# Four-layer attention kernel: half of the P V key tiles as three fp16 products, and the second output half ahead of the last score block

## The chip, the cores and the metric

The kernel runs on one core of one Trainium2 chip. The metric is the device time of one execution, in microseconds. The core's engines run side by side, each through its own instruction list in order, and wait for one another on semaphores: PE (TensorE), DVE (VectorE), ACT (ScalarE), POOL (GpSimd), and SP, which issues DMAs here.

## What is computed

Four attention layers, each added to the running `x` (4 batches, 512 queries, 256 channels), against one context of 1024 keys and 512 channels. Layers 0, 2 and 3 have 16 heads of 64 channels:

```python
q = hidden_states @ Wq
k = encoder_hidden_states @ Wk
v = encoder_hidden_states @ Wv
logits = jnp.einsum('bhqd,bhkd->bhqk', q, k) * scale
logits = logits + col_bias[None, None, :, :]
probs = jax.nn.softmax(logits, axis=-1)
out = jnp.einsum('bhqk,bhkd->bhqd', probs, v)
out = out @ Wo + bo
out = out + residual
```

Layer 1 is grouped attention (16 heads of 16 channels over 4 key/value heads) with an RMS norm of `x` in front. All of it is float32.

## The kernel before

The unit of work is a block `p`: one batch and two heads of a wide layer (96 blocks in layers 0, 2, 3), or one batch and four heads of layer 1 (16 grouped blocks); N = 112. Every engine has the same loop over slots `s`, written out by hand. A slot computes the scores of block `s`, the second half of P V, the sums and the output of block `s - 1`, and the projections of blocks `s + 1` and `s + 2`. Most slots of wide blocks are "turned" slots; their function is `turned_slot`.

Precision is kept by splitting a float32 number into two fp16 parts (`_h` and `_l`, on ACT the high part, on DVE or POOL the low part) and adding three products, high*high, high*low and low*high. P V alone is a plain float32 product: `attend` multiplies the exponentials `pt` (128 keys x 2 heads x 512 queries, a ring of RING = 6 places in SBUF) by the values `v32`, two heads side by side in the two column halves of the array.

The order in a turned slot of PE: score block 0 (line 981 the bias rows, line 930 the first "opening" maxima product, line 996 the scores of key tiles 0 and 1, line 930 the "closing" maxima product), `attend(s - 1, 1)` (line 1036, tiles 4 to 7), score block 1, sums (line 1056), projections of q, k and v (line 847), score block 2, `project_out(s - 1, 0)`, `attend(s, 0)` (tiles 0 to 3), score block 3, the second half of the next values v1 with the rows of maxima (line 939) in its middle, `project_out(s - 1, 1)`.

Around that order:

- An opening maxima product writes one bank of `ps_sm` and one of `ps_j`; the closing one writes the other bank of `ps_sm`, and with its second matmul the bank that the opening has just used. That matmul waits on `s_max_a`, that is until DVE has reduced the first half of the opening (`maxima`, line 1866: two instructions of 512 columns, each followed by the read-out of the accumulator).
- ACT takes the exponentials (line 1445) from PSUM into `pt`, copies projections out of PSUM (`values`, line 1426; `keys_hi`, line 1405), takes the high part of the summed exponentials (`sums_hi`, line 1452) and spreads the maxima (line 1489).
- POOL adds the eight exponentials of a block into `acc` (`add`, line 711, seven instructions), takes the low part of the sum (`sums_lo`, line 715), and normalizes and splits the output (lines 732 and 737).
- DVE does maxima, reciprocals, the low parts of k and q, and the additions into `x` (`add_out`, line 1911).
- The list `bank_users` gives each user of the two `ps_j` banks its turn; `take` makes PE wait until the reader of the bank's previous user is done.

## Time and profile before

| | us |
|---|---|
| median of 3 runs | 3505.33 (3504.23 to 3508.11) |
| the profiled execution, its own time | 3504.91 |
| its span, first to last instruction | 3502.7 |
| PE busy | 3365.6 (96%) |
| DVE busy | 2354.6 (67%) |
| POOL busy | 2187.3 (62%) |
| ACT busy | 1763.6 (50%) |
| additions of the exponentials, line 711, POOL (1365.5 and 223.2) | 1588.7 |
| P V matmuls of line 1036, PE, 3040 records | 694.2 |

The page gives the busy time of each engine and, for each line, the time that the engine stood idle before it and what ended that idle time. The timeline gives single instructions in order of time. A float32 matmul leaves two records. A matmul's duration includes the way through the array, so the spacing of starts tells what it costs in a row of matmuls.

### The profile page before, as it was taken

The numbers are of one execution on the slowest core, as the hardware profiler recorded it, in microseconds if no ns is written. First come the engines' busy times: TensorE is split into PE (matmuls) and PEld (weight loads), VectorE is DVE, ScalarE is ACT, GpSimd is POOL, SyncE is SP. The second block draws the span as 40 slices with busy tenths as digits, with TensorE's granted clock in tenths as the row PEclk, the third lists the DMA queues.
The fourth block names the chain that finished last, engine by engine and source line by source line (L and its number), as shares of the span: only waits on it lengthen the run. The fifth ranks groups of instructions, "written<-read, shape, count | busy, mean of one in ns | idle before, by whom it ended". The sixth has DMA issues, their size and how long they took to land.

```text
span 3502.7 us, 70154 instructions
## 1 busy us (share of the span) xinstructions
PE 3365.6 (96%) x27438; PEld 1545.0 (44%) x27438; DVE 2354.6 (67%) x4447; ACT 1763.6 (50%) x2228; POOL 2187.3 (62%) x1050
## 2 busy tenths in 40 slices
PE   5999999999997888889999999999999999999998
PEld 2444444444442322234444444444444444444443
DVE  5666666666656788856676666666666666666666
ACT  3444444444455677764444444444444444444444
POOL 5877777767650000028777776777787677767775
PEclk8999999999999999999999999999999999999999
DMA  4000000000000000000000000000000000000000
GB/s 144 10 10 10 1 10 10 9 3 9 6 10 10 9 12 17 17 1 10 10 1 10 10 10 1 10 10 9 3 10 10 1 10 10 10 1 10 3 1 25
DMA packets 50177, 42.09 MB, mean 12 GB/s; under 512 B 4928, under 2 KB 42176, under 8 KB 49856
## 3 DMA queue, kind: packets, MB, share of 16 engines
q1 hardware_dynamic: 49136, 37.08, 3.5%
q8 instruction: 225, 3.69, 0.4%
q14 instruction: 96, 0.79, 0.1%
q10 hardware_dynamic: 720, 0.53, 0.1%
HBM read 32.36 MB, written 2.10 MB: 10 GB/s over the span
## 4 chain that ended last, share of the span: by engine, by line
PE 89%; ACT 3%; DVE 3%; POOL 2%; issue 2%; DMA 0%; ACTq 0%; POOLq 0%; DVEq 0%
PE ps_j L847 39%; PE ps_j L1036 19%; PE ps_st L996 13%; PE ps_sm L930 6%; PE ps_st L981 3%; PE ps_j L1023 3%; ACT pt L1445 2%; PE ps_sm L1010 2%; POOL acc L711 2%; PE ps_j L1056 1%; PE ps_st L930 1%; PE ps_j L939 1%; PE ps_j L1072 0%; PE ps_j L1047 0%; DVE nmg L1856 0%
## 5 line engine op out<-in xcount | busy, mean ns | idle before, releaser
L711 POOL TENSOR_TENSOR acc<-acc,pt 128x1024 f32<-128x1024 f32 x570 | 1365.5, 2396 | 438.8 <-ACT pt L1445 385.1
L1445 ACT ACTIVATE pt<-ps_st 128x1024 f32<-128x1024 f32 x768 | 742.5, 1019 | 447.2 <-PE ps_st L996 435.4
L1036 PE MATMUL ps_j<-pt,v 128*64 128x512 f32 x3040 | 694.2, 598 | 1.4 <-DVE q_l L1771 1.3
L1866 DVE CUSTOM_DVE_ANT_0 ps_sm<-ps_sm,bias_m,nmx 128x512 f32<-128x512 f32 x666 | 480.1, 756 | 274.6 <-PE ps_j L930 227.7
L847 PE MATMUL ps_j<-w_h,ctx_h 128*128 128x128 f16 x3072 | 533.0, 220 | 1.6 <-ACT rinv L1461 1.1
L847 PE MATMUL ps_j<-w_l,ctx_h 128*128 128x128 f16 x3072 | 532.0, 220 | 0.0
L847 PE MATMUL ps_j<-w_h,ctx_l 128*128 128x128 f16 x3072 | 531.9, 220 | 0.0
L1866 DVE CUSTOM_DVE_ANT_0 ps_sm<-ps_sm,bias_m 128x512 f32<-128x512 f32 x486 | 334.4, 706 | 195.6 <-PE ps_j L930 186.4
L732 POOL TENSOR_TENSOR o_un<-o_un,rinv 128x512 f32<-128x512 f32 x111 | 141.6, 1275 | 485.5 <-ACT rinv L1457 294.9
L1036 PEld LDWEIGHTS ps_j<-pt,v 128*64 128x64 f32 x3040 | 201.8, 136 | 407.6 <-issue 369.6
L1903 DVE RECIPROCAL rinv<-rinv 128x256 f32<-128x256 f32 x190 | 331.2, 1745 | 11.2 <-ACT rinv L1461 1.6
L1856 DVE TENSOR_REDUCE nmg<-ps_st 128x2 f32<-128x1024 f32 x248 | 295.8, 1216 | 45.6 <-PE ps_st L930 44.4
L847 PEld LDWEIGHTS ps_j<-w_h,ctx_h 128*128 128x128 f16 x3072 | 301.3, 98 | 54.8 <-issue 40.1
L847 PE MATMUL ps_j<-ctx_h,w_h 128*128 128x512 f16 x800 | 305.1, 381 | 19.2 <-DVE w_l L1771 17.5
L1445 ACT ACTIVATE pt<-ps_sm 128x1024 f32<-128x1024 f32 x256 | 261.3, 1021 | 104.9 <-PE ps_sm L1010 104.8
L930 PE MATMUL ps_sm<-k_h,q_h 64*128 64x512 f16 x1160 | 294.3, 381 | 14.1 <-DVE nmx L1866 11.4
L847 PEld LDWEIGHTS ps_j<-w_l,ctx_h 128*128 128x128 f16 x3072 | 301.6, 98 | 10.7
L847 PE MATMUL ps_j<-ctx_l,w_h 128*128 128x512 f16 x800 | 304.8, 381 | 0.0
L847 PE MATMUL ps_j<-ctx_h,w_l 128*128 128x512 f16 x800 | 304.6, 381 | 0.0
L1405 ACT ACTIVATE k_h<-ps_j 128x512 f16<-128x512 f32 x192 | 114.6, 597 | 373.9 <-PE ps_j L847 373.9
L847 PEld LDWEIGHTS ps_j<-w_h,ctx_l 128*128 128x128 f16 x3072 | 301.6, 98 | 0.0
L996 PE MATMUL ps_st<-q_h,k_h 64*128 64x512 f16 x1488 | 282.4, 376 | 0.0
(182 smaller groups left out, 5490.0 us busy)
## 6 DMA issues: line engine op xcount, KB each, us to landing
w_raw<-wk SPq DMA_DIRECT2D x25, 256.0 KB, 2.8
pt<-ctx_t SPq DMA_DIRECT2D x6, 1024.0 KB, 8.1
w_raw<-wv SPq DMA_DIRECT2D x24, 256.0 KB, 3.6
wo_raw<-wo SPq DMA_DIRECT2D x28, 128.0 KB, 2.0
w_raw<-wq SPq DMA_DIRECT2D x24, 128.0 KB, 2.9
k_h<-k_l SPq DMA_DIRECT2D x72, 32.0 KB, 1.9
x<-x_t SPq DMA_DIRECT2D x4, 512.0 KB, 9.2
acc<-ctx_t SPq DMA_DIRECT2D x2, 1024.0 KB, 8.1
```

The source lines that it names most:

```text
L711: G.tensor_tensor(total, first, pt[:, n % RING, :], ALU.add).then_inc(s_acc, 1)
L732: G.tensor_tensor(o, o, rinv[:], ALU.mult).then_inc(s_o, 1)
L847: done = MM(dst, l, r, start=first and i == 0, stop=last and i == n - 1)
L930: last = MM(dst[h], queries_in(p, tile)[d, t * P:(t + 1) * P], k_h[d, r, half * HALF:(half + 1) * HALF], start=True, stop=True)
L981: MM(ps_st[:, j % 2, j // 2, :], ext_k[rows, buf, kt * P:(kt + 1) * P], ext_q[rows, p % 2, :], start=True, stop=False)
L996: last = MM(ps_st[:, side, h, :], k[d, r, keys], q[d, r, :], start=False, stop=n == 2)
L1036: last = MM(dst[h * HD:(h + 1) * HD, :], values_of(p)[:, kt, h * HD:(h + 1) * HD], pt[:, (units(p) + kt) % RING, h * TQ:(h + 1) * TQ], sta ...
L1405: A(k_h[:, r, keys], bank(f"k{half}", p), ACT.Copy, scale=1 / WS).then_inc(s_k_h, 1)
L1445: A(pt[:, n % RING, :], src.rearrange("p h q -> p (h q)"), ACT.Exp).then_inc(s_exp, 1)
L1856: V.tensor_reduce(nmg[:, half, t, 2 * tile:2 * tile + 2], maxima_in(p, u), AX_X, ALU.max, negate=True).then_inc(s_max, 1)
L1866: last = V.tensor_tensor_reduce(out=src, in0=src, in1=bias_m[:, t, half * HALF:(half + 1) * HALF], scale=-1.0, scalar=nmx[:, 0, t, h:h + 1 ...
L1903: V.reciprocal(r, r).then_inc(s_rinv, 1)
```

## The change

1. In 88 wide blocks (`in_terms`: 1 to 27 and 49 to 109) the key tiles 2, 3, 6 and 7 are multiplied in three fp16 products in place of one float32 product. For that ACT copies the high part of each such exponential tile (`probs_hi`), DVE (tiles 2, 6, 7) or POOL (tile 3) subtracts the low part (`probs_lo`), and half of the values are split too (`values_hi` on ACT, `values_lo` on DVE). The whole tile stands in the place two further in the ring and the two parts in its own, so `place_free` has more to wait for. The exponentials get a factor of 1024 through a bias.
2. `project_out(s - 1, 1)` goes from the end of the turned slot to just before score block 3, with its `add_out`, and the banks of what follows are swapped.
3. Start: the high part of the first two batches of `x` goes from POOL to ACT, DVE does a context split first and the token rows before the rest of its constants, POOL waits for the token rows, and in the first two slots the order of projections differs.
4. End: POOL adds the exponentials of tiles 0 to 3 of the last block, DVE those of tiles 4 to 7, and PE sums both.

```diff
+def in_terms(p):
+    return p >= 1 and turned(p - 1) and turned(p) and turned(p + 1)
@@ bank_users, turned slot
             then("pva", s, 0)
-            opening(3, 1)
-            if nxt:
-                then("v1", s + 1, 0)
-                then("nm0", s + 1, 1)
             if past:
                 then("out1", s - 1, 1)
+            opening(3, 0)
+            if nxt:
+                then("v1", s + 1, 1)
+                then("nm0", s + 1, 0)
@@ take
                     elif before in ("v0", "v1"):
                         pe.wait_ge(s_v_sb, values_before(m) + 1 + int(before[1]))
+                        if in_terms(m):
+                            pe.wait_ge(s_v_l, 2 * terms_before(m) + 1 + int(before[1]))
@@ attend
+                    if parted(p, kt):
+                        n = terms_before(p)
+                        if k == 2:
+                            pe.wait_ge(s_v_l, 2 * n + 1 + part)
+                        if kt == 3:
+                            pe.wait_ge(s_p_l_pool, n + 1)
+                        else:
+                            pe.wait_ge(s_p_l_dve, 3 * n + {2: 1, 6: 2, 7: 3}[kt])
+                        (vh, vl), (ph, pl) = value_parts(p, part), parts(p, kt)
+                        for i, (v, q) in enumerate(((vh, ph), (vh, pl), (vl, ph))):
+                            for h in range(2):
+                                last = MM(dst[h * HD:(h + 1) * HD, :], v[:, k - 2, h * HD:(h + 1) * HD],
+                                          q[:, h * TQ:(h + 1) * TQ], start=False, stop=k == 3 and i == 2)
+                        continue
@@ ACT
+            def values_hi(p, half):
+                act.wait_ge(s_v, values_before(p) + 1 + half)
...
+            def place_free(n, lent=True):
...
+                q, k = owner(n - 2)
+                if lent and not grouped(q) and parted(q, k):
+                    act.wait_ge(s_acc, ADDS * wides(q) + added(k))
+                    if k == 3:
+                        act.wait_ge(s_p_l_pool, terms_before(q) + 1)
+                    else:
+                        act.wait_ge(s_p_l_dve, 3 * terms_before(q) + {2: 1, 6: 2, 7: 3}[k])
+            def probs_hi(p, j):
+                act.wait_ge(s_exp, units(p) + j + 1)
+                place_free(units(p) + j)
+                A(parts(p, j)[0], whole(p, j), ACT.Copy).then_inc(s_p_h, 1)
@@ DVE
+            def values_lo(p, half):
+                dve.wait_ge(s_v_sb, values_before(p) + 1 + half)
...
+            def probs_lo(p, j):
+                dve.wait_ge(s_p_h, 4 * terms_before(p) + {2: 1, 6: 3, 7: 4}[j])
+                hi, lo = parts(p, j)
+                V.tensor_tensor(lo, whole(p, j), hi, ALU.subtract).then_inc(s_p_l_dve, 1)
```

Where the instructions stand now. DVE, from the end of one ordinary slot into the next, before (the two instructions on `ps_sm` and `ps_j` are the opening maxima of score block 0):

```order
L1887 SCALAR_TENSOR_TENSOR ext_q<-ps_j,flags_sb,bias_q 128x512 [waits s_st,s_nm]
L1911 SCALAR_TENSOR_TENSOR x<-ps_j,x 128x512 [waits s_x,s_out]
L1866 ISA ps_sm,nmx<-ps_sm,bias_m 128x512 [waits s_bias_sb,s_max_mm]
L1866 ISA nmx 128x1
L1866 ISA ps_j,nmx<-ps_j,bias_m 128x512
L1866 ISA nmx 128x1
L1866 ISA ps_sm,nmx<-ps_sm,bias_m,nmx 128x512 [waits s_max,s_bias_sb,s_nm16,s_max_mm]
```

and after:

```order
L2035 SCALAR_TENSOR_TENSOR ext_q<-ps_j,flags_sb,bias_q 128x512 [waits s_st,s_nm]
L2047 TENSOR_TENSOR pt<-pt 128x1024 [waits s_p_h]
L1919 SCALAR_TENSOR_TENSOR v<-ps_j,v 128x2x128 [waits s_v_sb]
L2014 ISA ps_sm,nmx<-ps_sm,bias_m 128x512 [waits s_bias_sb,s_max_mm]
L2014 ISA nmx 128x1
L2014 ISA ps_j,nmx<-ps_j,bias_m 128x512
L2014 ISA nmx 128x1
L2047 TENSOR_TENSOR pt<-pt 128x1024 [waits s_p_h]
L2014 ISA ps_sm,nmx<-ps_sm,bias_m,nmx 128x512 [waits s_max,s_bias_sb,s_nm16,s_max_mm]
```

The addition into `x` has gone from between the slots, and the low parts of tile 6 and of the values stand ahead of the opening maxima, the low part of tile 7 behind them.

ACT at the same place, before (line 1445 the exponentials of tiles 6 and 7, then the values, then the exponentials 0 and 1 of the next block, then the high part of the sum):

```order
L1489 ACTIVATE nm_w<-nmx 128x512 [waits s_max,s_nm]
L1445 ACTIVATE pt<-ps_st 128x1024 [waits s_acc,s_pva,s_st] x2
L1426 ACTIVATE v<-ps_j 128x512 [waits s_pvb,s_v]
L1445 ACTIVATE pt<-ps_st 128x1024 [waits s_acc,s_pva,s_st] x2
L1452 ACTIVATE sq<-acc 128x1024 [waits s_sum,s_acc]
```

and after:

```order
L1613 ACTIVATE nm_w<-nmx 128x512 [waits s_max,s_nm]
L1563 ACTIVATE pt<-ps_st,flags_sb 128x1024 [waits s_pva,s_st] x2
L1526 ACTIVATE v<-ps_j 128x2x128 [waits s_pvb,s_v]
L1569 ACTIVATE pt<-pt 128x1024 [waits s_acc,s_pva,s_exp]
L1512 ACTIVATE v<-ps_j 128x256 [waits s_pvb,s_v]
L1569 ACTIVATE pt<-pt 128x1024 [waits s_acc,s_pva,s_exp]
L1563 ACTIVATE pt<-ps_st,flags_sb 128x1024 [waits s_acc,s_p_l_dve,s_pva,s_st] x2
L1576 ACTIVATE sq<-acc 128x1024 [waits s_sum,s_acc]
```

The copy of tile 6 (line 1569) stands behind a copy of values that waits on `s_v`, and the exponentials of the next block wait on `s_p_l_dve` too.

PE from the end of score block 2 to score block 3, before:

```order
L930 MATMUL ps_sm<-k_h,q_h 128x512 [waits s_max_a]
L847 MATMUL ps_j<-o_h,wo_h 128x512 [waits s_v_sb,s_wo_l,s_o_l]
L847 MATMUL ps_j<-o_l,wo_h 128x512
L847 MATMUL ps_j<-o_h,wo_l 128x512
L1036 MATMUL ps_j<-pt,v 64x512 [waits s_max,s_v_sb,s_exp]
L1036 MATMUL ps_j<-pt,v 64x512 x7
L981 MATMUL ps_st<-ext_q,ext_k 128x512 [waits s_exp]
```

and after:

```order
L989 MATMUL ps_sm<-k_h,q_h 128x512 [waits s_max_a]
L906 MATMUL ps_j<-o_h,wo_h 128x512 [waits s_v_sb,s_v_l,s_wo_l,s_o_l]
L906 MATMUL ps_j<-o_l,wo_h 128x512
L906 MATMUL ps_j<-o_h,wo_l 128x512
L1109 MATMUL ps_j<-pt,v 64x512 [waits s_max,s_v_sb,s_exp]
L1109 MATMUL ps_j<-pt,v 64x512 x3
L1105 MATMUL ps_j<-pt,v 64x512 [waits s_p_l_dve,s_v_l]
L1105 MATMUL ps_j<-pt,v 64x512 x5
L1105 MATMUL ps_j<-pt,v 64x512 [waits s_p_l_pool]
L1105 MATMUL ps_j<-pt,v 64x512 x5
L906 MATMUL ps_j<-o_h,wo_h 128x512 [waits s_x,s_wo_l,s_o_l]
```

Four of the eight float32 matmuls have become twelve fp16 ones, the first output half waits on `s_v_l` as well, and the second output half follows at once.

## Rows read from the trace of the kernel before

**Rows 1.** The page, part 1: busy time, share of the span, instructions.

```profile
PE 3365.6 (96%) x27438; PEld 1545.0 (44%) x27438; DVE 2354.6 (67%) x4447; ACT 1763.6 (50%) x2228; POOL 2187.3 (62%) x1050
```

**Rows 2.** Busy time of each engine between 500 and 900 us.

```profile
500.00:900.00 400.00, 400.00 (x3367) 192.42 (x3365) 265.59 (x548) 189.13 (x246) 281.96 (x134) 1.00 0.02 7
```

**Rows 3.** Timeline of PE: start, duration, line, output and inputs, count.

```profile
604.09 0.40 PE L981 MATMUL ps_st<-ext_q,ext_k 32*128 32x512 f16 x4
...
609.11 0.22 PE L847 MATMUL ps_j<-w_h,ctx_l 128*128 128x128 f16 x1
...
609.91 0.40 PE L981 MATMUL ps_st<-ext_q,ext_k 32*128 32x512 f16 x4
...
611.76 0.38 PE L930 MATMUL ps_sm<-k_h,q_h 64*128 64x512 f16 x2
612.07 3.65 PE L1036 MATMUL ps_j<-pt,v 128*64 128x512 f32 x16
615.65 0.40 PE L981 MATMUL ps_st<-ext_q,ext_k 32*128 32x512 f16 x4
...
617.81 0.62 PE L1056 MATMUL ps_j<-sq,ones_h_sb 128*64 128x512 f16 x4
618.37 0.39 PE L847 MATMUL ps_j<-xh,w_h 128*128 128x512 f16 x1
...
642.10 3.65 PE L1036 MATMUL ps_j<-pt,v 128*64 128x512 f32 x16
```

**Rows 4.** Timeline of ACT, in the same slot.

```profile
606.97 1.92 ACT L1445 ACTIVATE pt<-ps_st 128x1024 f32<-128x1024 f32 x2
609.37 0.60 ACT L1426 ACTIVATE v<-ps_j 128x512 f32<-128x512 f32 x1 [0.48 <-PE ps_j L847]
...
613.14 1.06 ACT L1452 ACTIVATE sq<-acc 128x1024 f16<-128x1024 f32 x1
```

**Rows 5.** Timeline of POOL, in the same slot.

```profile
608.05 4.86 POOL L711 TENSOR_TENSOR acc<-acc,pt 128x1024 f32<-128x1024 f32 x2 [3.08 <-ACT pt L1445]
614.27 2.13 POOL L715 TENSOR_TENSOR sq<-acc,sq 128x1024 f16<-128x1024 f32 x1 [1.36 <-ACT sq L1452]
```

**Rows 6.** Timeline of DVE, opening maxima of score block 0.

```profile
610.67 0.70 DVE L1866 CUSTOM_DVE_ANT_0 ps_sm<-ps_sm,bias_m 128x512 f32<-128x512 f32 x1
611.29 0.14 DVE L1866 DVE_READ_ACCUMULATOR2_ANT nmx<- 128x1 f32 x1
611.29 0.73 DVE L1866 CUSTOM_DVE_ANT_0 ps_j<-ps_j,bias_m 128x512 f32<-128x512 f32 x1
```

**Rows 7.** Timeline of all engines at the start, DVE and POOL instructions.

```profile
24.52 5.00 POOL L688 TENSOR_TENSOR ctx_l<-pt,ctx_h 128x2048 f16<-128x2048 f32 x1 [2.94 <-ACT ctx_h L1366]
25.64 4.97 DVE L1826 SCALAR_TENSOR_TENSOR v_rms<-iota_sb,tok_f,v_rms 128x1024 f16<-128x1024 f16 x1
...
29.49 5.03 POOL L688 TENSOR_TENSOR ctx_l<-acc,ctx_h 128x2048 f16<-128x2048 f32 x1
...
30.64 4.96 DVE L1828 SCALAR_TENSOR_TENSOR ext_k<-y_rms,flags_sb,v_rms 128x1024 f16<-128x1024 f16 x1
```

**Rows 8.** Instructions by line: count, min/median/max ns, first and last start.

```profile
L1779 DVE TENSOR_TENSOR ctx_l<-pt,ctx_h x2: 2277/2281/2285, 12.9 to 17.3; 128x2048 f16<-128x2048 f32 x2
L1395 ACT ACTIVATE wo_h<-wo_raw x28: 408/417/417, 97.0 to 3413.1; 128x256 f16<-128x256 f32 x28
```

**Rows 9.** Timeline of PE around two holes, in the grouped layer and at the end.

```profile
1086.84 0.59 PE L847 MATMUL ps_j<-o_h,wo_h 128*128 128x512 f16 x1 [3.92 <-DVE x L1911]
...
1096.47 0.38 PE L1010 MATMUL ps_sm<-q_l,k_h 64*128 64x512 f16 x2
...
3490.12 1.08 PE L1309 MATMUL ps_sm<-acc,ones_sb 128*64 128x512 f32 x4 [2.82 <-DVE acc L2114]
...
3492.22 0.38 PE L847 MATMUL ps_j<-o_l,wo_h 128*128 128x512 f16 x1
```

**Rows 10.** Timeline of PE at the start.

```profile
36.47 1.18 PE L1089 MATMUL ps_j<-ext_k,bias_q 32*128 32x512 f16 x2 [10.58 <-DVE k_l L1771]
```

More of the change, by code:

```diff
@@ L175, in splits_x, with terms_before, parted @@
     return p < N and not grouped(p) and p - STARTS[layer_of(p)] < B
+def in_terms(p):
+    return p >= 1 and turned(p - 1) and turned(p) and turned(p + 1)
+def terms_before(p):
+    return sum(in_terms(i) for i in range(p))
+def parted(p, kt):
+    return in_terms(p) and kt in TERM_TILES
 def place_of(p, u):
@@ L525, in values_of, with whole, parts, value_parts @@
             return v32[:, b if grouped(p) else p % 2]
+        def whole(p, kt):
+            return pt[:, (units(p) + kt + (2 if parted(p, kt) else 0)) % RING, :]
+        def parts(p, kt):
+            both = pt[:, (units(p) + kt) % RING, :].bitcast(F16)
+            return both[:, 0:2 * TQ], both[:, 2 * TQ:4 * TQ]
+        def value_parts(p, half):
+            both = v32[:, p % 2, half * 4 + 2:half * 4 + 4, :].bitcast(F16)
+            return both[:, :, 0:P], both[:, :, P:2 * P]
         def maxima_in(p, u):
@@ L706, in add @@
                         pool.wait_ge(s_pv, KT * (groups(p) + p - G1 - 1))
-                    first = pt[:, (n - 1) % RING, :]
+                    first = whole(p, 0)
                 else:
@@ L710, in add, with probs_lo @@
                     first = total
-                G.tensor_tensor(total, first, pt[:, n % RING, :], ALU.add).then_inc(s_acc, 1)
+                G.tensor_tensor(total, first, whole(p, kt), ALU.add).then_inc(s_acc, 1)
+            def probs_lo(p):
+                pool.wait_ge(s_p_h, 4 * terms_before(p) + 2)
+                hi, lo = parts(p, 3)
+                G.tensor_tensor(lo, whole(p, 3), hi, ALU.subtract).then_inc(s_p_l_pool, 1)
             def sums_lo(p):
@@ L741, in last_slot @@
                 sums_lo(q)
+                for kt in range(1, 4):
+                    n, total = units(N - 1) + kt, acc[:, (N - 1) % 2, :]
+                    pool.wait_ge(s_exp, n + 1)
+                    if kt == 1:
+                        pool.wait_ge(s_sum, N - 2)
+                        first = pt[:, (n - 1) % RING, :]
+                    else:
+                        pool.wait_ge(s_end_add_g, kt - 1)
+                        first = total
+                    G.tensor_tensor(total, first, pt[:, n % RING, :], ALU.add).then_inc(s_end_add_g, 1)
                 normalize(q)
@@ L1124, in wide_slot @@
                     rows_of_reciprocals(s - 1)
[L1125 to L1131 removed]
+                if s < 0:
+                    if s == -1:
+                        project_k(s + 2, 0)
+                    project_q(s + 2, 0)
+                    score_block(2)
+                    project_k(s + 2, 1)
+                else:
+                    if nxt and has_values(s + 1):
+                        project_v(s + 1, 0)
+                    if far:
+                        project_k(s + 2, 1)
+                        if not late_queries(s):
+                            project_q(s + 2, 0)
+                    score_block(2)
                 if past:
@@ L1306, in last_sums @@
             def last_sums():
-                pe.wait_ge(s_end_add, ADDS)
-                for h in range(2):
-                    last = MM(end_sum[h * HD:(h + 1) * HD, :], ones[:, 0:HD], acc[:, (N - 1) % 2, h * TQ:(h + 1) * TQ],
-                              start=True, stop=True)
+                pe.wait_ge(s_end_add_g, 3)
+                for i in range(2):
+                    if i:
+                        pe.wait_ge(s_end_add, 3)
+                    for h in range(2):
+                        last = MM(end_sum[h * HD:(h + 1) * HD, :], ones[:, 0:HD],
+                                  acc[:, (N - 1 + i) % 2, h * TQ:(h + 1) * TQ], start=i == 0, stop=i == 1)
                 last.then_inc(s_end_sum, 1)
@@ L1627, in turned_slot @@
                     group_out(s - 1)
+                if s > 0 and in_terms(s - 1):
+                    probs_hi(s - 1, 7)
                 exponentials_of(0)
@@ L1639, in turned_slot @@
                     queries_hi(s + 2)
-                    if not splits_x(s):
-                        keys_hi(s + 2, 0)
+                if termed:
+                    probs_hi(s, 2)
+                if far and not splits_x(s):
+                    keys_hi(s + 2, 0)
+                if termed:
+                    probs_hi(s, 3)
+                if far:
                     keys_hi(s + 2, 1)
@@ L1644, in turned_slot @@
                     output_hi(s - 1)
+                if nxt and in_terms(s + 1):
+                    values_hi(s + 1, 0)
                 if nxt:
@@ L1654, in turned_slot @@
                 exponentials_of(3)
+                if nxt and in_terms(s + 1):
+                    values_hi(s + 1, 1)
+                if termed:
+                    probs_hi(s, 6)
                 if nxt:
@@ L1931, in _ @@
             link(V.tensor_tensor(tok_f[:], tok_f[:], tok_w, ALU.add))
+            weights_lo(0)
+            for step in range(5):
+                token_rows(0, step)
+            context_lo(1)
             link(V.tensor_scalar(mask_t, mask_t, -1.0, 1.0, ALU.mult, ALU.add))
@@ L1963, in wide_slot @@
                 peak()
-                if far:
+                if s != -1 and far:
                     keys_lo(s + 2, 0)
-                if s == -2:
-                    dve.wait_ge(s_init, 1)
-                    for step in range(5):
-                        token_rows(0, step)
                 peak()
@@ L2002, in turned_slot @@
                 peak()
+                if s > 0 and in_terms(s - 1):
+                    probs_lo(s - 1, 7)
                 peak()
@@ L2027, in turned_slot @@
                 peak()
+                if nxt and in_terms(s + 1):
+                    values_lo(s + 1, 0)
                 peak()
@@ L2036, in turned_slot @@
                     extra_rows(s + 1)
-                if past:
-                    add_out(s - 1, 1)
+                if in_terms(s):
+                    probs_lo(s, 6)
+                if nxt and in_terms(s + 1):
+                    values_lo(s + 1, 1)
             def group_slot(s):
```

169 lines of the change are left out of this document (110 added, 59 removed).

## The prediction

> **What bounds the kernel now.** I read the page's busy times first: PE 96%, DVE 67%, POOL 62%, ACT 50% [rows 1]. Then the windows: between 500 and 900 us PE is busy 400.00 of 400 us at clock 1.00 [rows 2]. The wide blocks therefore run at PE's own pace, and no other engine is late for it. Then one slot in the timeline: P V starts at 612.07 and again at 642.10 [rows 3], so a slot is 30.03 us. In such a slot fewer PE cycles are a gain only as long as nobody else becomes late, so the question for each edit is what it puts in front of an instruction that PE waits for. Last I read the other engines where one slot meets the next [rows 4 to 6].
>
> **P V itself.** Four float32 key tiles take 615.65 - 612.07 = 3.58 us, of which some 0.1 is the change of tile shape, so 0.87 a tile. Two fp16 pairs of the same shape (the sums) take 618.37 - 617.81 = 0.56, that is about 0.22 a pair and a change-over [rows 3]. Three products are 0.65 a tile. Each converted tile saves 0.22, four a block 0.87, and 88 blocks 76 us. The trace shows no step from float32 to fp16 in one tile shape: its cost is between 0 and the 0.1 of a shape change, once for each half, so 0 to 18 us in all. I take 0, the same shape being kept.
>
> **The end of the slot.** The new work on ACT and DVE is small in sum (four copies of 1.06 [rows 4] and about three subtractions of 1.15 a slot, on engines with more than 9 us free), but its place counts. I take the times of the slot at 609.91 and leave out the output half that no longer stands between v1 and the next slot; v1 ends as before (last start 609.11), and the next score block starts near 609.27 instead of 609.91 [rows 3].
>
> - ACT can copy values when v1 is done, at 609.37 [rows 4]. The copy of tile 6 is queued behind `values_hi`, which waits for v1. `values_hi` has 256 columns: 0.42 by the nearest row [rows 8], of which the next instruction overlaps 0.1. `probs_hi` of tile 6 starts near 609.67 and takes the 1.06 of the same shape on line 1452 [rows 4]: 610.73.
> - DVE may then subtract tile 6, near 610.76. It reads two SBUF operands. The trace shows what such an instruction does beside POOL: line 1826 starts at 25.64 while POOL works, and ends at 30.61, 1.1 us after POOL's instruction (24.52 + 5.00 = 29.52); line 1828 does the same against the next one, and that POOL instruction in turn has its end at 34.52 [rows 7]. So DVE waits for the running POOL instruction to end. POOL's two last additions run from 608.05 to 612.91 [rows 5], the second from about 610.48: it is running when DVE comes. DVE gets through at 612.91 and needs 2.28 / 2 = 1.15 [rows 8]: 614.05.
> - `values_lo` reads one operand from PSUM, half of the 0.6 to 0.7 of a 512-column instruction plus its start, 0.4: 614.4.
> - Then the opening maxima: its first half is read out 0.76 after its start [rows 6]: 615.2.
> - The second matmul of the closing product waits for exactly this. PE issues it at 611.76 in a slot that begins at 609.91 [rows 3], so at 611.1 now. It stands until 615.2: a hole of **4.1 us** in every slot that follows a converted block. The rest of PE's queue stands behind it.
>
> The Trainium skill bears on the second step (SBUF — State Buffer, section "Who interferes with whom"): a VectorE instruction with two SBUF inputs and a GpSimd instruction that reads SBUF exclude each other for a whole instruction, and one with at most one SBUF input does not take part. The trace agrees with the first half (4.97 us on a 1.1 us instruction). By the second half `values_lo` and the maxima do not wait for POOL; the sum takes them so, from rows 6, where the maxima run at their own length beside POOL's additions.
>
> **Two more waits in the same slot.** The ring place of exponential 1 of the next block is lent to tile 7 of this one, so that exponential waits for the low part of tile 7. Both opening halves end at 614.4 + 1.5 = 615.9, the low part of tile 7 at 617.05, the exponential (1.02) at 618.1, the high part of the sum at 619.1, and its low part on POOL (2.13 [rows 5]) at 621.25. PE, after the hole: 615.2 + 0.3 + 3.15 of P V + 2.16 of score block 1 = 620.8. It waits 0.5 for the sums. Before, this chain had 1.4 us in hand (614.27 + 2.13 against 617.81). And the first output half takes the bank of v0, which now is free only after `values_lo`, behind the opening maxima of score block 2: these end some 0.1 after the score block does (612.17 against 612.07 in block 0 [rows 3, 6]), and 0.4 more gives a wait of **0.5**. The second output half ahead of score block 3 costs PE nothing: it covers ACT's copy out of the bank that the block needs next.
>
> **The sum.** A slot is 30.03 - 0.87 + 4.1 + 0.5 + 0.5 = 34.3, or 4.2 more; 88 of them are 370 us. In 21 slots (every fourth, with the weight split) the additions of POOL start later and it is a toss-up whether DVE comes first; in 10 more (the first blocks of a layer, where POOL adds `bo`) the wait is about 1.2 shorter: together -29. The two ends: 10.58 us at the start pass while PE waits behind DVE's token rows, which are themselves stretched by POOL [rows 7, 10]; the new order lets them run first and alone. At the end PE waits 2.82 for DVE's additions [rows 9], which are now shared. I take -11 for both, with bounds -3 and -16.
>
> **The clock.** After the hole of 3.92 us at 1086.84 the matmuls of 512 columns take 0.59 to 0.63 in place of 0.38, until 1096.47: the lower of the two levels (1.2 in place of 2.4 GHz) for 9.5 us. After 2.82 us of waiting at 3490.12 they take 0.38 as ever [rows 9]. A hole of 4.1 is on the wrong side. Each drop costs half of the slow stretch: between 0 (it does not come) and 4 us (as at 1086.84) a slot. In full work I expect less than there, about 2.5, not in each slot, and some of it in place of the wait for the sums: 1.25 a slot, 110 us.
>
> 3504.91 + 370 - 29 + 110 - 11 = **3945 us**; the profiled execution stands 0.4 below the median, which changes nothing.
>
> **The rivals.**
>
> 1. *DVE comes ahead of POOL's last addition.* The margin is 610.76 against 610.48, 0.3 us, and rests on durations of instructions that the trace does not show. Then tile 6 is subtracted by 611.9, the opening's first half is read by 613.0, and the hole is 1.9. POOL's addition is pushed back instead, and with it the low part of tile 7 and the sums, a wait of about 0.9 to 1. A slot costs 1.9 + 1.0 + 0.5 - 0.87 = 2.5 more: 3505 + 220 - 11 = 3714; without the wait for the sums 3626. Such a hole is shorter than the 2.82 that left the clock alone.
> 2. *The saving stands (faster).* This needs DVE to be at the opening maxima by 610.4, before PE's closing matmul. The tail between v1's end and that point is 0.3 + 1.06 + 1.15 + 0.4 and would have to fit into 1.0 us: both new instructions on `pt` in less than a third of their nearest rows (1.06 and 2.28 / 2). From there on PE stays full: 3505 - 76 - 11 = 3418, up to 3436 with the type changes. For it speaks only that PE is 96% busy and the others have room.
> 3. *The change does not do what it says:* the fp16 products of the two heads do not run side by side. Then P V takes 12 x 0.22 a half in place of 1.74, 0.9 more, and a slot 2.6 more than in my sum. The pairs of the sums [rows 3] speak against it. It would give about 4150.
>
> **How the numbers follow.** The forecast, a hole near 4 us with the clock somewhere between never and always down, spans 3800 to 4110: 68%. Rival 1, 3626 to 3800: 22%. Rival 2: 5%. No change within 0.2% (7 us, about what a measurement of this kernel can tell) would need the saving and the waits to cancel: 2%. Above 4110, rival 3 or a clock that is down most of the time: 3%. The range of 8 in 10 takes the forecast and most of rival 1: 3650 to 4110. Faster 5%, same 2%, slower 93%.
>
> **What the changed profile would show.** PE's waits: a matmul of the maxima (line 989 there) waiting for DVE's maxima some 88 times, about 4 us each (1.9 in rival 1, none in rival 2). DVE's subtraction of `pt` (line 2047) at 1.15 where POOL is idle and near 3.3 for tile 6. P V's fp16 pairs 0.22 apart. PE's wait for the low part of the sum, and for `values_lo` ahead of the first output half, 0.5 each. PE's clock below 1.00 in the slices of the wide layers. The step most likely to be wrong is the 0.3 us between DVE and POOL; the next is how often the clock falls.

## The result, and the profile after

| kernel | us, median (lowest to highest) | runs | span of the profiled run | mean granted clock |
|---|---|---|---|---|
| before | 3505.49 (3504.23 to 3508.11) | 4 | 3502.7 | 0.992 |
| after | 3935.38 (3934.0 to 3936.35) | 4 | 3932.1 | 0.956 |

After is 1.1226 times before, 95% interval 1.1212 to 1.1239. The change makes the kernel 430 us slower. The forecast was 3945.

The page of after, busy times, against [rows 1]: PE has fewer cycles to do in P V, and yet is busy longer (its clock) and for a smaller share (holes).

```profile
PE 3492.5 (89%) x28146; PEld 1609.8 (41%) x28146; DVE 2800.6 (71%) x4884; ACT 2185.0 (56%) x2758; POOL 2472.3 (63%) x1138
```

PE's waits in after (what PE was about to do, for whom, us in total, times, longest). Of the first, 11.4 us were there in before.

```profile
PE ps_sm L989 <- DVE nmx L2014: 261.5, 96, 3.6
PE ps_j L906 <- DVE v L1919: 29.4, 81, 0.4
PE ps_j L1129 <- POOL sq L762: 21.4, 25, 0.9
```

One boundary between slots, PE first (start, length, engine, line, operation; in brackets the idle time before it and who ended it), against [rows 3]:

```profile
614.47 0.39 PE L1040 MATMUL ps_st<-ext_q,ext_k 32*128 32x512 f16 x4
...
616.32 0.38 PE L989 MATMUL ps_sm<-k_h,q_h 64*128 64x512 f16 x1
620.33 0.60 PE L989 MATMUL ps_sm<-k_h,q_h 64*128 64x512 f16 x1 [3.64 <-DVE nmx L2014]
620.87 3.68 PE L1109 MATMUL ps_j<-pt,v 128*64 128x512 f32 x8
624.33 2.24 PE L1105 MATMUL ps_j<-pt,v 128*64 128x512 f16 x12
```

The same stretch on ACT, DVE and POOL, against [rows 4 to 6]:

```profile
614.57 0.38 ACT L1526 ACTIVATE v<-ps_j 128x256 f16<-128x256 f32 x1 [0.29 <-PE ps_j L906]
614.85 1.05 ACT L1569 ACTIVATE pt<-pt 128x1024 f16<-128x1024 f32 x1
```

```profile
615.93 3.35 DVE L2047 TENSOR_TENSOR pt<-pt 128x1024 f16<-128x1024 f32 x1 [1.95 <-ACT pt L1569]
619.20 0.41 DVE L1919 SCALAR_TENSOR_TENSOR v<-ps_j,v 128x256 f16<-128x256 f32 x1
619.54 0.68 DVE L2014 CUSTOM_DVE_ANT_0 ps_sm<-ps_sm,bias_m 128x512 f32<-128x512 f32 x1
```

```profile
613.35 4.84 POOL L752 TENSOR_TENSOR acc<-acc,pt 128x1024 f32<-128x1024 f32 x2 [2.50 <-ACT pt L1563]
```

The second of POOL's two additions, alone:

```profile
615.85 2.34 POOL L752 TENSOR_TENSOR acc<-acc,pt 128x1024 f32<-128x1024 f32 x1
```

Read from the bottom up. POOL adds tiles 6 and 7 from 613.35 to 618.19. ACT has the high part of tile 6 ready at 615.90. DVE starts to subtract it at 615.93, only 0.08 us after POOL began its last addition, and ends at 619.28, which is 1.1 us after POOL's end. So it was let through when POOL's instruction ended. The same instruction takes 1.21 to 1.22 where no instruction of POOL runs beside it. Only then come the values' low part and the maxima. PE could have issued the second closing product beside the first, at 616.32; it issues it at 620.33, and 4.01 us are lost. The matmuls after the hole take 0.60 in place of 0.38: the clock has fallen to its lower level.

In the next slot, one with a weight split, DVE comes 0.13 us before POOL's last addition. Then DVE keeps its own length, POOL's addition takes 3.31 in place of 2.34 us, and PE's hole is 1.45:

```profile
652.70 1.23 DVE L2047 TENSOR_TENSOR pt<-pt 128x1024 f16<-128x1024 f32 x1 [1.95 <-ACT pt L1569]
```

```profile
652.83 3.31 POOL L752 TENSOR_TENSOR acc<-acc,pt 128x1024 f32<-128x1024 f32 x1
```

The clock by stretches: the 30 us from the block with the long hole, the next slot (whose hole is 1.45), and the middle of the wide layers (columns: stretch, its length, PE, PEld, DVE, ACT and POOL busy, granted clock, DMA), against [rows 2]:

```profile
614.40:644.80 30.40, 26.40 (x188) 11.38 (x185) 20.96 (x36) 16.37 (x21) 20.33 (x10) 0.89 0.00 1
644.80:680.00 35.20, 32.51 (x281) 15.78 (x279) 26.27 (x50) 19.73 (x27) 28.36 (x13) 1.00 0.08 24
```

```profile
500.00:900.00 400.00, 357.34 (x2977) 172.33 (x2977) 286.57 (x532) 217.53 (x280) 280.06 (x126) 0.96 0.03 7
```

### The profile page after: what moved, and what is told of

The parts are those of the page before. It is cut to its first block, busy times and chain, and to the rows that moved or that the text cites. A ratio compares the mean times of both kernels' runs of the same rounds, so it can differ in the third digit from the quotient of the medians.

```text
span 3932.1 us, 73857 instructions
## 1 busy us (share of the span) xinstructions
PE 3492.5 (89%) x28146; PEld 1609.8 (41%) x28146; DVE 2800.6 (71%) x4884; ACT 2185.0 (56%) x2758; POOL 2472.3 (63%) x1138
## 4 chain that ended last, share of the span: by engine, by line
PE 52%; POOL 20%; issue 14%; DVE 7%; ACT 6%; DMA 0%; ACTq 0%; DVEq 0%; POOLq 0%; SPq 0%
PE ps_j L906 25%; POOL acc L752 12%; PE ps_j L1109 8%; PE ps_j L1105 4%; PE ps_st L1055 3%; PE ps_sm L989 3%; PE ps_j L1082 3%; POOL sq L762 2%; DVE ps_sm L2014 2%; POOL o_un L779 2%; ACT pt L1557 2%; POOL pt L758 1%; PE ps_sm L1069 1%; PE ps_st L1040 1%; ACT pt L1563 1%
## 5 line engine op out<-in xcount | busy, mean ns | idle before, releaser
L752 POOL TENSOR_TENSOR acc<-acc,pt 128x1024 f32<-128x1024 f32 x570 | 1401.2, 2458 | 284.3 <-ACT pt L1563 232.8
L1563 ACT ACTIVATE pt<-ps_st,flags_sb 128x1024 f32<-128x1024 f32 x768 | 831.0, 1109 | 676.3 <-DVE pt L2047 290.3
L2047 DVE TENSOR_TENSOR pt<-pt 128x1024 f16<-128x1024 f32 x264 | 458.8, 1738 | 170.2 <-ACT pt L1569 170.2
L989 PE MATMUL ps_sm<-k_h,q_h 64*128 64x512 f16 x1160 | 341.7, 389 | 267.4 <-DVE nmx L2014 261.5
L779 POOL TENSOR_TENSOR o_un<-o_un,rinv 128x512 f32<-128x512 f32 x111 | 214.3, 1931 | 458.5 <-ACT rinv L1581 295.2
L1109 PE MATMUL ps_j<-pt,v 128*64 128x512 f32 x1632 | 483.4, 725 | 1.4 <-DVE q_l L1919 1.3
L762 POOL TENSOR_TENSOR sq<-acc,sq 128x1024 f16<-128x1024 f32 x92 | 196.5, 2136 | 434.7 <-ACT sq L1576 434.7
L1569 ACT ACTIVATE pt<-pt 128x1024 f16<-128x1024 f32 x352 | 369.0, 1050 | 0.0
L2070 DVE SCALAR_TENSOR_TENSOR x<-ps_j,x 128x512 f32<-128x512 f32 x222 | 152.3, 686 | 218.2 <-PE ps_j L906 217.9
L906 PEld LDWEIGHTS ps_j<-w_l,ctx_h 128*128 128x128 f16 x3072 | 302.0, 98 | 10.7
```

Source lines behind the costliest of these rows:

```text
L752: G.tensor_tensor(total, first, whole(p, kt), ALU.add).then_inc(s_acc, 1)
L779: G.tensor_tensor(o, o, rinv[:], ALU.mult).then_inc(s_o, 1)
L906: done = MM(dst, l, r, start=first and i == 0, stop=last and i == n - 1)
L989: last = MM(dst[h], queries_in(p, tile)[d, t * P:(t + 1) * P], k_h[d, r, half * HALF:(half + 1) * HALF], start=True, stop=True)
L1109: last = MM(dst[h * HD:(h + 1) * HD, :], values_of(p)[:, kt, h * HD:(h + 1) * HD], pt[:, (units(p) + kt) % RING, h * TQ:(h + 1) * TQ], sta ...
L1563: A(whole(p, j), ps_st[:, j % 2].rearrange("p h q -> p (h q)"), ACT.Exp, bias=flags[:, FLAG_PS:FLAG_PS + 1]).then_inc(s_exp, 1)
```

## The experiments

All of them stand beside runs of the kernel before on the same chip (3505.0 to 3505.9 us).

| kernel | us | ratio to before (95%) | longest PE wait for the maxima, and its total |
|---|---|---|---|
| after | 3935.4 | 1.1226 (1.1212 to 1.1239) | 3.6, 261.5 |
| one_input | 3890.1 | 1.1088 (1.1073 to 1.1103) | 3.1, 214.5 |
| pool_yields | 3774.5 | 1.0764 (1.075 to 1.0779) | 2.6, 145.1 |
| maxima_first | 3759.0 | 1.0731 (1.0713 to 1.0749) | (wait is elsewhere) |
| act_first | 3725.8 | 1.0632 (1.0614 to 1.0649) | 2.6, 122.3 |
| reduce_input | 3696.4 | 1.0543 (1.0527 to 1.0559) | 2.6, 138.9 |
| tiles_2_3_early | 3551.1 | 1.0132 (1.0117 to 1.0147) | 2.8, 33.1 |
| tiles_2_3 | 3532.5 | 1.0083 (1.0068 to 1.0098) | 2.6, 11.8 |
| no_terms | 3522.7 | 1.0047 (1.0033 to 1.0061) | 2.6, 11.4 |
| no_terms_no_bias | 3510.8 | 1.0014 (1.0005 to 1.0023) | 2.6, 11.5 |
| products_only | 3435.8 | 0.9802 (0.9788 to 0.9815) | 1.7, 11.4 |
| ends_only, tiles_2_3_plain | 3636.0, 3645.6 | 1.0369, 1.0396 | see below |

Where the longest wait is 2.6, it stands once, near 57 us at the start; the holes at the boundaries between slots are given with each kernel.

### Is the saving there? products_only

The kernel before, with this in `attend`:

```diff
+                    if in_terms(p) and k >= 2:
+                        ctx = (ctx_h[:, batch_of(p), 0, :], ctx_l[:, batch_of(p), 0, :])
+                        for i, (x, y) in enumerate(((0, 0), (0, 1), (1, 0))):
+                            for h in range(2):
+                                last = MM(dst[h * HD:(h + 1) * HD, :], ctx[x][:, k * P + h * HD:k * P + (h + 1) * HD],
+                                          ctx[y][:, h * TQ:(h + 1) * TQ], start=False, stop=k == 3 and i == 2)
+                        continue
```

> The kernel before with the 12 fp16 products of each half in place of two float32 tiles, read from the context's tiles, which are there from the start: P V's real values are left out, and no copy, subtraction or wait is added. Mine: the products alone save 0.87 us a block, 88 blocks, 3429 us (up to 3447 with a price for the step between the types). Rival (PE is full, but a faster P V only meets another engine sooner): 3480 to 3505.

Measured 3435.8: 69.8 us less than before. A half of P V in it, from PE's timeline (five more pairs stand ahead of the last line, 0.22 apart):

```profile
599.67 1.94 PE L1048 MATMUL ps_j<-pt,v 128*64 128x512 f32 x8
601.43 0.39 PE L1044 MATMUL ps_j<-ctx_h 128*64 128x512 f16 x2
...
602.83 0.39 PE L986 MATMUL ps_st<-ext_q,ext_k 32*128 32x512 f16 x4
```

602.83 - 599.67 is 3.16 in place of 3.58 [rows 3]: 0.42 for two tiles, 0.84 for a block. The saving is real, nothing else in the kernel stops it, and it is nearly as large as the sum had it (76). The loss comes from what makes the operands, but for the 17 us that no_terms shows below.

### What is the hole? one_input, reduce_input, pool_yields

Three edits of after. In the first two, DVE's instruction for tile 6 is another one, with one SBUF input; in the third, POOL's last addition waits.

```diff
 one_input
+                if j == 6:
+                    V.tensor_scalar(lo, whole(p, j), 1.0, None, ALU.mult).then_inc(s_p_l_dve, 1)
+                    return
 reduce_input
+                if j == 6:
+                    V.tensor_reduce(lo, whole(p, j).rearrange("p (n o) -> p n o", o=1), AX_X, ALU.max
+                                    ).then_inc(s_p_l_dve, 1)
+                    return
 pool_yields, in POOL's add
+                if kt == 7 and in_terms(p):
+                    pool.wait_ge(s_p_l_dve, 3 * terms_before(p) + 2)
```

> The changed kernel; DVE's subtraction for tile 6 is replaced by a multiplication by 1.0 that reads one SBUF tile alone (the subtraction of the high part is left out, so the values of P V are wrong for that tile); all waits are the same, and POOL keeps its place. Theory P with the limit to two SBUF inputs: the instruction takes 1.15 us or less beside POOL, the hole falls to 1.5 to 1.9, and POOL's additions keep their time: 3600 to 3720 us. If any DVE instruction on SBUF tiles waits for POOL: 3.3 us as before, and 3935. Theory L: it falls only by what the instruction itself is shorter than 1.15.

> The changed kernel; DVE's subtraction for tile 6 is replaced by a reduction over pairs of one element (a copy in effect), which reads one SBUF tile alone and is as long as the subtraction; the high part isn't subtracted, so that tile's P V is wrong. All waits stay. Theory P with two inputs as the condition: about 1.2 us beside POOL's addition, PE's hole before the closing product 1.5 us in place of 3.6, POOL's last addition as early as after, so no longer wait for the sums: 3660 to 3720 us, below the kernel where POOL yields (3774). If one input is enough to be shut out: 3935.

> The changed kernel; POOL's last addition of a converted block waits until DVE has subtracted tile 6. Theory P (DVE's subtraction waits for the running addition's end): the subtraction takes 1.15 in place of 3.35 us, PE's hole before the closing product falls from 3.6 to about 1.5 to 1.9 us, the addition ends 1.2 us later and the sums with it; 3630 to 3760 us, the clock at 1.00 nearly everywhere. Theory L (the hole is the length of the four new instructions of ACT and DVE in a row, and POOL has no part): the hole stays at 3.6, 3935 us or above.

one_input missed: 3890 and not 3600 to 3720. The summary of its line, and then of reduce_input's (times, and shortest, median and longest in ns):

```profile
L2048 DVE TENSOR_SCALAR pt<-pt x88: 694/2806/2818, 127.4 to 3823.6; 128x1024 f16<-128x1024 f32 x88
```

```profile
L2048 DVE TENSOR_REDUCE pt<-pt x88: 1219/1220/1221, 126.5 to 3629.1; 128x1024 f16<-128x1024 f32 x88
```

The multiplication is a 0.69 us instruction, yet its median is 2.81 beside POOL: it is shut out as the subtraction is, by 2.1 us. So "one SBUF input" alone was the wrong condition, and the edit, meant to test it, had an instruction that is also much shorter than the subtraction (0.69 against 1.22 us). The reduction runs at the subtraction's pace, with one input, and takes 1.22 us in all 88 blocks, POOL's additions running beside it (606.87 to 611.72 in one slot, the reduction from 609.24). By the Trainium skill (SBUF — State Buffer, "Who interferes with whom") `tensor_scalar` can enter a two-port mode, in which it takes the port pair that it shares with GpSimd, while `tensor_reduce` never contends on trn2. The two rows above agree with both; that `tensor_scalar` was in such a mode is seen here only in its pace. The same section makes its rule on one SBUF input for instructions outside these modes; the prediction's sentence on it left that condition out, and one_input was built on the short form.

With the reduction the hole is 1.44 us, the clock is 1.00 between 500 and 900 us, and the kernel takes 3696, within 3660 to 3720. Only DVE's blocked instruction has changed, so being shut out, and what follows from it, are 239 of the 430 us: PE's idle time before the maxima's product falls by 123, and most of the rest is the clock (0.992 in place of 0.956). The wait for the sums did not become shorter: it is 34.4 us, 0.4 in 84 blocks, since PE now comes sooner. And the shorter hole remains. PE still issues the closing product 1.8 us late (609.69 to 611.51), with POOL no longer in the way: ACT's two copies and DVE's two low parts stand ahead of the maxima. pool_yields shows the same from the other side. Its DVE and its POOL:

```profile
623.89 1.23 DVE L2049 TENSOR_TENSOR pt<-pt 128x1024 f16<-128x1024 f32 x1 [1.95 <-ACT pt L1571]
```

```profile
621.51 2.36 POOL L754 TENSOR_TENSOR acc<-acc,pt 128x1024 f32<-128x1024 f32 x1 [1.59 <-ACT pt L1565]
625.25 2.35 POOL L754 TENSOR_TENSOR acc<-acc,pt 128x1024 f32<-128x1024 f32 x1 [1.38 <-DVE pt L2049]
```

The subtraction takes 1.23 in place of 3.35, the hole is 1.45, and 1.38 us now pass on POOL. That is not free: PE's wait for the sums grows from 21.4 us to this, 0.8 in 79 blocks:

```profile
PE ps_j L1131 <- POOL sq L764: 64.8, 79, 0.9
```

PE also waits 19.6 us for exponentials at score block 1. 3774 is above the 3760 that I gave as its bound. Theory L, that the four new instructions in a row are the hole, is left with the 1.4 us that remain in both.

### Which order? act_first, maxima_first

```diff
 act_first, in ACT's turned_slot
+                if termed:
+                    probs_hi(s, 6)
                 if nxt and in_terms(s + 1):
                     values_hi(s + 1, 1)
-                if termed:
-                    probs_hi(s, 6)
 maxima_first, in DVE's turned_slot; both calls go from the end of the slot before
                 peak()
+                if s > 0 and in_terms(s):
+                    values_lo(s, 1)
+                peak()
                 if s > 0 and in_terms(s - 1):
+                    probs_lo(s - 1, 6)
                     probs_lo(s - 1, 7)
-                peak()
```

> The changed kernel; ACT copies the high part of tile 6 before the high part of the values, so DVE comes to its subtraction 0.5 us earlier, near 615.4 where POOL's sixth addition still runs (it ends at 615.8). Theory P, with DVE taking the port where POOL's addition ends, as in the rows of the start: the subtraction runs from 615.8 to 617.0, the hole is about 1.5 to 2 us, POOL's last addition ends 1.1 us later; 3700 to 3790 us, like the kernel where POOL yields (3774). If POOL goes on to its next addition with DVE waiting: 3935 as after.

> The changed kernel; DVE does the opening maxima of the next block before it takes the low parts of the values and of tiles 6 and 7. Theory P with PE's order as the cause: the hole before the closing product goes, P V waits for the low parts instead, by 1 to 2.5 us, since two float32 tiles run before they are needed; 3620 to 3760 us. Rival (the wait is as long wherever it stands, since the same chain ends in the same sums): above 3850.

act_first gave 3726. DVE comes 0.5 us earlier, which is before POOL's first addition ends, and gets through between the two. DVE and POOL of one slot:

```profile
614.33 1.53 DVE L2047 TENSOR_TENSOR pt<-pt 128x1024 f16<-128x1024 f32 x1 [1.48 <-ACT pt L1569]
```

```profile
612.43 5.64 POOL L752 TENSOR_TENSOR acc<-acc,pt 128x1024 f32<-128x1024 f32 x2 [1.59 <-ACT pt L1563]
```

POOL's pair takes 5.64 in place of 4.84, DVE's instruction 1.53 in place of 3.35. Two lines in another order on ACT, whose own work is the same, are worth 210 us. It is rival 1 of the prediction: 3714 was its time. PE issues the closing product 1.66 us late (615.26 to 616.92), where the rival had 1.9, and the wait for the sums is 65.0 us, 0.8 in 79 blocks.

The clock is 1.00 between 500 and 900 us, but it fell behind some holes of this kernel that are shorter than the 2.82 us that the prediction called harmless. The eight float32 matmuls of P V take 1.94 at the full clock, and 3.24 here; the granted clock between 2785 and 2792 us is 0.76:

```profile
2785.65 0.39 PE L989 MATMUL ps_sm<-k_h,q_h 64*128 64x512 f16 x1 [1.73 <-DVE nmx L2014]
2785.97 3.24 PE L1109 MATMUL ps_j<-pt,v 128*64 128x512 f32 x8
```

maxima_first gave 3759, at the top of its range. PE's waits:

```profile
PE ps_j L1129 <- POOL sq L762: 77.1, 84, 0.9
PE ps_j L1105 <- DVE pt L2047: 68.8, 168, 1.6
...
PE ps_st L1040 <- ACT pt L1563: 33.8, 85, 0.7
```

The hole ahead of the closing product is gone; its shorter successors stand in P V (0.4 a time, twice a block), at score block 1 and at the sums. The clock is at 0.993.

### How much without the tail? tiles_2_3, tiles_2_3_early

`TERM_TILES = (2, 3)`, with all that makes parts of tiles 6 and 7 and of the second values' half taken out. In the second kernel also, on DVE:

```diff
+                if nxt and in_terms(s + 1):
+                    values_lo(s + 1, 0)
                 peak()
-                if nxt and in_terms(s + 1):
-                    values_lo(s + 1, 0)
                 peak()
```

> The changed kernel with tiles 2 and 3 converted and 6 and 7 left in float32: nothing new stands between the values' second half and the next block. Against the kernel with nothing converted (3523): half of the saving that the products alone showed (70 / 2 = 35), and a wait of 0 to 0.4 us a slot for the values' low part before the first output half: 3488 to 3523. Rival (part of the loss sits in the first half's copies and subtractions as well): above 3560.

> As the kernel with tiles 2 and 3 alone; DVE takes the values' low part before the opening maxima of score block 2, so that the first output half finds its bank free. Mine: PE's 0.36 us wait of each slot before that half goes, 3485 to 3492. Rival (DVE then comes late to the opening maxima by as much): no gain over the kernel with tiles 2 and 3 alone.

Both missed, on the same side: 3532.5 and 3551.1, where no_terms is 3522.7. In the second, the rival (no gain) came. Half of the conversion, in the place where no hole comes, gains nothing. PE around the first output half in tiles_2_3, and the line in tiles_2_3_early that has the wait instead:

```profile
631.00 0.38 PE L989 MATMUL ps_sm<-k_h,q_h 64*128 64x512 f16 x2
631.74 0.38 PE L906 MATMUL ps_j<-o_h,wo_h 128*128 128x512 f16 x1 [0.36 <-DVE v L1913]
```

```profile
635.23 0.39 PE L989 MATMUL ps_sm<-k_h,q_h 64*128 64x512 f16 x1 [0.17 <-DVE nmx L2008]
```

631.74 - 631.00 is 0.74, and 0.31 without the wait (629.18 to 629.49 in no_terms): 0.43 us lost against 0.42 saved in P V right behind it. In the second kernel the closing product's two matmuls stand at 634.68 and 635.23, where they could stand side by side: 0.55 lost. DVE and PE keep step here, maxima for maxima, so that a 0.4 us instruction on DVE costs PE as much on either side of them. 88 x 0.12 is 11 of the 19 us between the two kernels. Of the other 8, and of the 10 between tiles_2_3 and no_terms, the traces show the place: compared by the low parts of the sum on POOL, block for block, 5.8 of the 10 and 4.7 of the 8 pass where the last layer begins (2490 to 2650 us in no_terms), and the ordinary slots of tiles_2_3 lose less than 3 us together. What waits there, and why, stays open.

### The small terms: no_terms, no_terms_no_bias, ends_only, tiles_2_3_plain

```diff
 no_terms
 def in_terms(p):
-    return p >= 1 and turned(p - 1) and turned(p) and turned(p + 1)
+    return False
 no_terms_no_bias: also
-              bias=flags[:, FLAG_PS:FLAG_PS + 1]).then_inc(s_exp, 1)
+              ).then_inc(s_exp, 1)
 ends_only: also the second output half back, with this line in bank_users
+                then("out1", s - 1, 0)
```

> The changed kernel with no block converted: the ends and the second output half ahead of score block 3 stay. My theory (the ends give 11 us, the moved output half nothing): 3494 us, 3489 to 3502. Rival (the moved output half takes part in the loss of 430 us, by putting PE in front of a late o_l or of DVE's maxima): 3505 or more, up to 3600 if it costs 1 us a slot.

> The changed kernel with no block converted and without the bias operand of the wide blocks' exponentials (no factor 1024). Theory B: the operand makes each exponential 0.09 us longer (2.12 in place of 1.94 for two), ACT copies the sums 0.14 later, and PE waits 0.14 a slot for their bank before the keys: about 110 slots, so 3522.7 falls to 3507. Rival: the 17 us above the kernel before come from the moved output half alone: 3522.

> As the last, and the second output half back behind the values' second half: what is left of the change is the two ends. Mine: the extra change of tile shape (0.11 us a slot) goes too: 3494 us, 3490 to 3498, faster than the kernel before. Rival (the ends give nothing): 3505.

> Tiles 2 and 3 converted, no bias operand, the second output half at its old place, the new ends. PE saves 0.43 in P V's first half and waits 0.43 for the values' low part before the first output half: 3494 to 3505 us, no better than the kernel with the ends alone. If the two cancel less in this order: down to 3470.

no_terms missed its range (3489 to 3502) and came in its rival's: it is slower than before (3522.7, the ratio's interval is above 1), so there are costs that I had put at nothing. The low part of the sum is an instruction of POOL in nearly every wide block; its first and its last place but one, of before, of no_terms and of no_terms_no_bias:

```profile
104.53 2.13 POOL L715 TENSOR_TENSOR sq<-acc,sq 128x1024 f16<-128x1024 f32 x1
...
3447.35 2.13 POOL L715 TENSOR_TENSOR sq<-acc,sq 128x1024 f16<-128x1024 f32 x1 [1.37 <-ACT sq L1452]
```

```profile
100.17 2.12 POOL L762 TENSOR_TENSOR sq<-acc,sq 128x1024 f16<-128x1024 f32 x1
...
3464.35 2.13 POOL L762 TENSOR_TENSOR sq<-acc,sq 128x1024 f16<-128x1024 f32 x1 [1.17 <-ACT sq L1576]
```

```profile
98.12 2.13 POOL L762 TENSOR_TENSOR sq<-acc,sq 128x1024 f16<-128x1024 f32 x1
...
3451.68 2.13 POOL L762 TENSOR_TENSOR sq<-acc,sq 128x1024 f16<-128x1024 f32 x1 [1.17 <-ACT sq L1575]
```

At the first place no_terms_no_bias is 6.4 us ahead: the new order of the start. At the other it is 4.3 behind, so what is left of the change, the moved output half, costs 10.7 us over the slots, 0.11 a slot. The likely cause is that P V, output half, scores is one change of tile shape more than P V, scores; no run tests that alone. no_terms is 17.0 behind there, another 12.7: the bias operand. An exponential of the wide blocks takes 1019 ns in before and 1108 in no_terms (the form's mean in both), and what comes of it stands on ACT and on PE, where the keys' bank is given back by the copy of the sums:

```profile
616.63 2.12 ACT L1563 ACTIVATE pt<-ps_st,flags_sb 128x1024 f32<-128x1024 f32 x2 [2.31 <-PE ps_st L1055]
618.63 0.60 ACT L1585 ACTIVATE rinv<-ps_j 128x512 f32<-128x512 f32 x1
```

```profile
619.02 0.38 PE L906 MATMUL ps_j<-xh,w_l 128*128 128x512 f16 x1
619.38 0.38 PE L906 MATMUL ps_j<-ctx_h,w_h 128*128 128x512 f16 x1
```

The same pair in before:

```profile
619.46 0.38 PE L847 MATMUL ps_j<-xh,w_l 128*128 128x512 f16 x1
619.67 0.38 PE L847 MATMUL ps_j<-ctx_h,w_h 128*128 128x512 f16 x1
```

0.36 between these two in place of 0.21. With the operand gone 3522.7 fell to 3510.8, which shows this cause; 3507 was 4 us low, and the rival's 3522 is out. The cost of the moved output half is what is left over between the two places, not a run of its own.

ends_only and tiles_2_3_plain don't tell what they were made for. Before has the second output half in bank 1; my edit put it in bank 0, the bank of the values' second half that PE has just filled. PE's waits in ends_only:

```profile
PE ps_j L906 <- ACT v L1516: 71.6, 92, 0.8
PE ps_sm L989 <- DVE x L2069: 48.4, 89, 0.6
```

120 us of waits for one wrong digit in a table of banks. The kernel with only the ends of this change was thus not measured, and the expectations of 3494 and of 3494 to 3505 are neither met nor refuted. By the places above it would be near 3505.5 - 6.4 = 3499; that is an estimate. The pair still agrees on one point: with tiles 2 and 3 converted it is 9.6 us slower than without, as tiles_2_3 is 9.8 slower than no_terms.

## Why the prediction was right, point by point

The forecast case came, in its place and by its mechanism. The tail, counted from the start of score block 0 (609.27 in the prediction, 614.47 in after):

| event | predicted | measured |
|---|---|---|
| high part of tile 6 ready | 1.46 | 1.43 |
| POOL's last addition begins | 1.21 | 1.38 |
| DVE comes to subtract it | 1.49 | 1.46 |
| POOL's last addition ends | 3.64 | 3.72 |
| tile 6 subtracted | 4.78 | 4.81 |
| values' low part done | 5.13 | 5.14 |
| PE issues the closing product | 5.93 | 5.86 |

The lost time is 5.93 - 1.83 = 4.1 by the prediction (1.83 is where the product could have gone, 611.1 - 609.27) and 4.0 in the trace. But the 0.3 us by which POOL was to be first were 0.08 to 0.1 in 53 of the 54 slots with the long hole. The prediction took POOL's second addition to begin halfway through the pair, at 610.48; the trace of before has it at 610.55, and in after it begins 0.17 later than predicted. act_first, which turns just this order, shows that it was worth 210 us. That the forecast case came and not rival 1 is therefore partly luck: the working could not tell 0.1 us either way.

The sum, term by term (us, on the profiled executions):

| term | predicted | measured | from |
|---|---|---|---|
| P V | -76 | -70 to -74 | products_only; 88 x 0.84 |
| hole, special slots taken off | +361 - 29 | +283 | 261.5 - 11.4, and 88 x 0.37 |
| wait for the sums | +44 | +21 | PE's waits |
| wait of the first output half | +44 | +29 | PE's waits |
| ends | -11 | -6 | first low part of the sum; the spans add nothing at the other end |
| moved output half, bias operand | 0 | +23 | 10.7 + 12.7 |
| clock | +110 | +136 to +145 | below |

- **The hole** is 3.63 to 3.65 (idle time; 0.37 more is lost, since the matmul before it runs alone) in 54 of the 88 boundaries, 1.45 in 20, between 1.7 and 2.3 in 11, and shorter in 3. The 20 are slots with a weight split, where ACT and POOL are shifted against each other. The prediction called them a toss-up; all of them went DVE's way, by 0.12 to 0.13 us. Against 88 x 4.01 the shorter holes take off 70 us, 44 of them in these 20; the 29 taken off was too little by 41.
- **The clock.** Of its two levels one is half of the other, so the time at the lower is 2 x (1 - clock) x span: 56 us before, 346 after. Half of the difference, 145, is lost at most; with PE's idle time inside the slow stretches left out it is 136. It fell behind each of the 54 holes of 3.6 us, and behind most of those of 3.1 in one_input (0.95 between 500 and 900 us); pool_yields, act_first and reduce_input, with holes of 1.2 to 1.5 there, and maxima_first, with waits below 1 us, have 1.00 in the same stretch. The prediction's reading of [rows 9], that 3.92 us brings the clock down and 2.82 does not, gave the right side for this hole, but the length of a hole alone does not decide: in act_first the clock fell behind holes of 1.73 (2785.65) and 1.72 us (194.20). 1.25 us a slot was low: 1.55 to 1.65 came.
- **The output half "costs PE nothing"** failed by 0.11 a slot, and the bias operand of the exponentials wasn't in the sum. The row was there: two exponentials take 1.94 in before [rows 4], and nothing in it tells what an operand more costs. I should have bounded it.
- **The waits** came where they were expected, at 0.87 and 0.36. The wait for the sums came in 25 slots only, and none of them has the long hole. The prediction had it behind the long hole too, and in full: with 3.15 us for P V, PE would come 0.5 early. Behind the 54 long holes P V took 4.4 to 6.1 us at the lower clock, so PE came when the sums were ready. The prediction allowed for this exchange only in its clock term.
- **The rule on one SBUF input**, as the prediction gives it, is too wide: one_input has one and was shut out. The sum isn't touched, since `values_lo` and the maxima read from PSUM and ran at 0.41 and 0.68 us.
- **Rival 1** came in the 20 slots, and nearly everywhere in act_first. **Rival 2** (the saving stands) is out: it takes a P V whose operands cost nothing, as in products_only. **Rival 3** is out: a half of P V got 0.42 shorter, not 0.9 longer. (Its time should have been 3945 + 88 x 2.6 = 4174, not 4150; nothing hangs on that.)

The measured terms add up to 421 to 425 (412 to 416 with the clock at 136), against 429.4 between the spans; 4 to 17 us are not accounted for. The costs of the operand and of the moved output half are taken from kernels without conversion, and no run shows them in after. The hole and the two waits were too large by 87, the clock, the ends, P V, the operand and the moved output half too small by 56 to 69, so that 3945 comes so near to 3935 is luck: errors of both signs cancelled.

## What to carry to other kernels

Before work is moved off a full engine to engines with time to spare, ask between which two instructions of theirs it lands, and whom the full engine waits for there: here 1.6 us of DVE work, behind ACT's copies, cost PE 4.0. Of these, 2.2 came from an addition that the third engine had begun 0.08 us before; 1.8 remain with the reduction, which isn't shut out. And 0.4 us of DVE work elsewhere cost PE 0.4 and ate a saving of 0.42. If a step runs beside GpSimd, prefer an instruction of DVE that isn't shut out, or arrange that it arrives at a boundary between GpSimd's instructions; the order of two instructions on a third engine can decide that. Undo a change in parts: the two small edits that rode along cost 23 us, more than the start's new order gave.

## What the runs showed of the hardware that was not expected

- `tensor_scalar` with one SBUF input is shut out by POOL like the subtraction (median 2.81 us for a 0.69 us instruction); `tensor_reduce` is not (1.219 to 1.221 us, 88 times). I had expected that one input is enough to stay clear of POOL.
- A DVE instruction that waits for POOL gets through where POOL's current instruction ends, ahead of POOL's next: POOL's two additions take 5.64 in place of 4.84 in act_first, and DVE's instruction 1.53. When it comes 0.08 us after the last addition has begun it takes 3.35, and when it comes 0.13 before it, POOL's addition is the one that waits (3.31 in place of 2.34).
- A bias operand makes ACT's exponential of 128x1024 0.09 us longer (1019 and 1108 ns, 768 of each).
- The clock is still high at the first matmul after 8 of the 54 holes of 3.6 us (0.39 at 689.74 in after, 0.60 at 620.33), and falls in the P V right behind it (3.09 us for its eight float32 matmuls, 1.94 at full clock). It also fell behind single holes of 1.7 us, with the first matmul behind them still at 0.39.
